# LN2's rows turned on VectorE in 32x32 blocks and carried by 16 small transfers, in a fused attention and FFN kernel

## The chip, the cores and the metric

The kernel runs on one core of a Trainium2 chip. The metric is device time in microseconds (us), the median of several executions. Everything is in float32; a product is made of three TensorE matmuls on "high" and "low" parts of both operands (the high part is rounded to the format that TensorE multiplies in one pass, the low part is the rest).

## What is computed

For each of 16 batches of 512 rows with 512 features, with a context of 77 rows:

```
hc = layernorm(x)                                  # LN1, no gain or bias
sim = hc@w1 + ctx@w2 + (hc*w3)@ctx.T + b_sim ;  A = softmax(sim)
hq = A@ctx ; hbar = softmax(rowmax(sim)) @ hc
x = x + [hc, hq, hc*hq, hc*hbar] @ W_qv + b_qv     # 2048 -> 512
h = layernorm(x) @ W1 + b1                         # LN2, 512 -> 2048
q = h + 0.1*(cos(th)*wr + sin(th)*wi) * wi * sin(th + 0.1*h)
x = x + relu(q) @ W2 + b2                          # 2048 -> 512
```

The change concerns the step from layernorm(x), LN2, to the operand of `@ W1`: TensorE needs the features on the partitions, LN2 has the rows there, so the 512x512 tile has to be turned.

## The kernel before

One program is written by hand for every engine, with counting semaphores between them; the order on each engine is that of the text. The loop is over batches b (0 to 15) and, in each, over 16 tiles f of 128 hidden features. In step f TensorE (PE) makes `hidden(b, f)` (12 matmuls, W1's tile as the weights and `T` as the moving operand) and `second(b, f-3)` (12 matmuls with W2's tile). ScalarE (ACT) reads the PSUM tile `hid` twice (`phase_and_hidden`: `ph`, `h2`), takes the high part of relu (`relu_high`) and the sine; VectorE (DVE) does `reduce_phase`, `sine_term`, `relu_low`. GpSimd (POOL) streams the split weights from DRAM and makes the small row statistics (`moments`). In batch 0 the weights come raw through SyncE's queue (SP), and ACT and DVE split them beside all else (`tile_high`, `tile_low`); SP loads a raw tile only when the low part of the tile two before it is made.

Under the FFN of batch b the attention of batch n = b+1 is made: its large products are put in at f = 10 and 11 (NA = 10), and DVE adds them to `X` (`attention_and_stats`) at f = 11. Then LN2 of batch n follows: `norm_second(n, t)` normalises 128 rows into `xin` on DVE, `tr_second(n, t)` turns them on PE by four 128x128 transposes into the PSUM tile `mis`, `turned_high` (ACT) and `turned_low` (DVE) write them into the half of `T` of the other parity. Rows t = 0, 1 go at f = 13, rows 2, 3 at f = 14. `hidden(n, 0)` waits for `t2_lo`, that is for all of it, at the start of the next batch. `turn_stats(n+1)` is one PE transpose of LN1's statistics for the batch after, at the end of f = 12; `stat_rows` copies it out on ACT, and `spread_stats` sends it over DRAM to all partitions through SP's queue. `ctx_raw` holds the raw context rows of a batch; SP loads it (`ctx_load`) after `spread_stats`.

Of the kernel before, what the change touches and what calls it, by code (L numbers as in the profile page):

```python
# [34 lines left out]
F32 = mybir.dt.float32  # L35
# [15 lines left out]
def xattn_ffn(nc, x, ctx_rows, w_sim, b_sim, W_qv, b_qv, W1, W2, b2, x_turned, ctx_turned, columns, out):  # L51
# [36 lines left out]
    with ExitStack() as ctx:  # L88
# [128 lines left out]
        x2_done = sem("x2_done"); xb2_done = sem("xb2_done")  # L217
        st2 = sem("st2"); mo2 = sem("mo2"); rs2 = sem("rs2"); xn2 = sem("xn2"); tr2 = sem("tr2")
        t2_hi = sem("t2_hi"); t2_lo = sem("t2_lo")
# [110 lines left out]
        x0n = w0_sb  # L330

        g_view = g_raw.rearrange("p (c j) -> p c j", c=C)

# [4 lines left out]
        def _(sp):  # L338
            row = lambda v, n: v.rearrange("(a d) -> a d", a=1).to_broadcast([n, D])

            def x_load(n):

                need(sp, out_stored, 16 * (n - 2))
                sp.dma_start(X[:, n % 3], x_rows[n]).then_inc(x_in, 16)

            def turned_load(n):
# [45 lines left out]
            def ctx_load(n):  # L392

                sp.wait_ge(pr_lo, C * n)
                sp.wait_ge(w0_lo, C * n)
                sp.wait_ge(att_done, RT * n)
                last = chunk_of_row(n * J + J - 1)
                for k in range(chunk_of_row(n * J), last + 1):
                    if k < GAP:
                        sp.wait_ge(p_stored[k % 4], 16 * (k // 4 + 1))  # L400
                    else:
                        sp.wait_ge(p_late[k - GAP], 16)
                g_load(n, ctx_in)
                stack_load(n, hq_raw, hq_tail, ctx_flat, ctx_in)
                stack_load(n, hqw_raw, hqw_tail, hqw_dram, ctx_in)
# [70 lines left out]
            def body(b, par, first, last):  # L476
                n, pn = b + 1, 1 - par
                for f in range(FT):
# [26 lines left out]
                    if f == (NA + 3 if first else NA + 2):  # L505
                        spread_stats(n + 1)

            def rest():
# [9 lines left out]
        def _(pe):  # L518
# [48 lines left out]
            def hidden(b, f, par):  # L567

                g = FT * b + f
                w1_ready(b, f)  # L570
                need(pe, h2_done, g - 1)
                if f == 0:
                    pe.wait_ge(t2_lo, RT * (b + 1))
                if b == 0 and f < 2:
                    pe.wait_ge(c_copy, CN - GAP - 1 + f)
                w = w1s[:, f % NW1]
                for c in range(C):
                    three(hid[:, f % 2], w[:, 0, c], w[:, 1, c], T[:, par, 0, c], T[:, par, 1, c],
                          c == 0, c == C - 1, hid_done if c == C - 1 else None)
# [53 lines left out]
            def sim_rows(n):  # L633
                pe.wait_ge(simt_done, n + 1)
                for t in range(RT):
                    tr = pe.transpose(mis[:, 1, t * J:(t + 1) * J], simt[:, t * P:(t + 1) * P], ident[0:J, 0:J])
                tr.then_inc(simr_done, 1)
# [109 lines left out]
            def body(b, par, first, last):  # L747
                n, pn = b + 1, 1 - par
                for f in range(FT):
# [18 lines left out]
                    if f == NA + 1 and not last:  # L768
                        continue
                    if f == NA + 2 and not last:  # L770
                        second(b, NA - LAG, False)
                        second(b, NA - LAG + 1, False)
# [6 lines left out]
                    if f == NA - 1:  # L779
                        hq_hat(n, 0)  # L780
                    if f == NA + 2 and n + 1 < B:
                        turn_stats(n + 1)
# [15 lines left out]
        def _(sc):  # L798
            def turned_high(n, t, par, ready, done):
                sc.wait_ge(ready, RT * n + t + 1)  # L800
                nc.scalar.copy(T[:, par, 0, :, t * P:(t + 1) * P],
                               mis[:, t % 2].rearrange("p (c r) -> p c r", c=C)).then_inc(done, 1)

            def spread_high(n, c, par):
# [71 lines left out]
            def phase_and_hidden(b, f):  # L876
# [3 lines left out]
                need(sc, q_done, g - 1)  # L880
                nc.scalar.activation(ph[:, f % 2], hid[:, f % 2], ACT.Identity, bias=hbias[:, f:f + 1],  # L881
                                     scale=HSCALE).then_inc(t_done, 1)
                need(sc, act_lo, g - 1)
                nc.scalar.activation(h2[:, f % 2], hid[:, f % 2], ACT.Identity, bias=b1c[:, f:f + 1],  # L884
                                     scale=1.0).then_inc(h2_done, 1)
# [110 lines left out]
            def body(b, par, first, last):  # L996
                n, pn = b + 1, 1 - par
                for f in range(FT):
# [14 lines left out]
                    if f == NA and not last:  # L1013
                        w0_high(n, 1)
                    phase_and_hidden(b, f)
                    if first and f < FT - 3:
                        w1_high(f + 3)
# [27 lines left out]
                    if f == (5 if first else 6):  # L1045
                        max_exponentials(n)
                    if f == NA + 2 and n + 1 < B:
                        stat_rows(n + 1)
                    if f == NA - 1:
# [22 lines left out]
        def _(ve):  # L1072
# [257 lines left out]
            def attention_and_stats(n, tiles=range(RT)):  # L1330

                for t in tiles:
# [3 lines left out]
                    ve.bn_stats(st[:, t], X[:, n % 3, t]).then_inc(st2, 1)  # L1336

            def norm_second(n, t):
                ve.wait_ge(rs2, t // 2 + 1 if isinstance(n, int) and n == 0 else n + 2)
                if t >= 2:  # L1340
                    ve.wait_ge(tr2, RT * n + t - 1)
                ve.tensor_scalar(xin[:, t % 2], X[:, n % 3, t], mv[:, t, 1:2], rstd[:, t:t + 1],
# [106 lines left out]
            def body(b, par, first, last):  # L1449
                n, pn = b + 1, 1 - par  # L1450
                for f in range(FT):
# [10 lines left out]
                    if f == NA + 3 and not last:  # L1462
                        norm_second(n, 0)
                        norm_second(n, 1)
                    if f == NA + 4 and not last:
                        norm_second(n, 2)
                        norm_second(n, 3)
                    reduce_phase(b, f)
# [58 lines left out]
                    if first:  # L1527
                        for p in splits(f, last)[0:1] if f == NA else splits(f, last):
                            tile_low(p)
                    if (f > 0 or not first) and not early:  # L1530
                        relu_low(g - 1, (f - 1) % FT)
# [17 lines left out]
                    if f == NA + 1:  # L1549
                        attention_and_stats(n)  # L1550
                    if f == NA + 3:
                        turned_low(n, 0, pn, t2_hi, t2_lo)
                        turned_low(n, 1, pn, t2_hi, t2_lo)
                    if f == NA + 4:
                        turned_low(n, 2, pn, t2_hi, t2_lo)
                        turned_low(n, 3, pn, t2_hi, t2_lo)

# [176 lines left out]
```

## Time and profile before

| | |
|---|---|
| median of 3 runs | 1956.96 us (1955.17 to 1958.2) |
| profiled execution: its time, its span | 1955.15 us, 1953.3 us |
| PE, DVE, ACT, POOL busy, share of the span | 99%, 71%, 51%, 21% |
| TensorE's granted clock over the run | 0.998 of full speed |

The profiled execution's own time lies 1.8 us below the median. Matmuls overlap in the records (a 512-column matmul is listed with 0.39 us and the next starts 0.23 us later), so times of PE are read from start to start.

### The profile page before, as it was taken

Reading aid. Unit: us, or ns where it says so; the run is one execution under the profiler, and the core shown is the slowest. Engines: PE = TensorE matmul, PEld = TensorE weight load, DVE = VectorE, ACT = ScalarE, POOL = GpSimd, SP = SyncE. Lnnn points to the kernel's source line nnn. Section 1 sums busy time; section 2 is a strip of 40 time slices with the busy share of each in tenths; the row PEclk is TensorE's granted clock in tenths of the full one; section 3 lists DMA queues with packets and bytes.
Section 4 is the critical chain, followed back from the end, with each engine's and each line's share of the span. In section 5 each row is a group of like instructions: output and inputs, shape, how many; then the busy total and the mean of one; then the engine's idle time right before and its main releaser. Section 6 shows DMA issues by size and latency. Waiting matters only on the chain.

```text
span 1953.3 us, 24524 instructions
## 1 busy us (share of the span) xinstructions
PE 1938.4 (99%) x8709; PEld 1585.8 (81%) x8709; DVE 1379.2 (71%) x2377; ACT 990.4 (51%) x1676; POOL 408.4 (21%) x834
## 2 busy tenths in 40 slices
PE   8999999999999999999999999999999999999999
PEld 7778788888888888888888888888888888888887
DVE  7888786766777676776766867667776667767554
ACT  5574645536365363644636455363653636446343
POOL 1223121131211212112121211312122121221210
PEclk9999999999999999999999999999999999999999
DMA  8587857577574875757667475774748757576463
GB/s 258 175 282 244 263 160 238 171 229 226 161 224 141 254 233 164 212 175 226 203 202 222 158 232 166 233 228 159 222 149 253 225 172 213 170 225 189 151 216 119
DMA packets 144279, 397.63 MB, mean 204 GB/s; under 512 B 22380, under 2 KB 35416, under 8 KB 142238
## 3 DMA queue, kind: packets, MB, share of 16 engines
q0 software_dynamic: 83568, 304.29, 49.9%
q1 hardware_dynamic: 60446, 91.74, 15.6%
q8 instruction: 71, 1.16, 0.2%
q14 instruction: 50, 0.41, 0.1%
q10 hardware_dynamic: 144, 0.04, 0.0%
HBM read 355.50 MB, written 38.30 MB: 202 GB/s over the span
## 4 chain that ended last, share of the span: by engine, by line
PE 93%; DVE 3%; ACT 2%; issue 1%; DMA 0%; SPq 0%; DVEq 0%; ACTq 0%
PE acc L521 18%; PE acc L523 17%; PE acc L522 17%; PE hid L521 11%; PE hid L523 11%; PE hid L522 11%; PE mis L607 1%; PE acc L529 1%; PE mis L529 1%; PE acc L530 1%; PE mis L530 1%; PE mis L523 1%; PE mis L521 1%; PE mis L522 1%; DVE ph L1225 0%
## 5 line engine op out<-in xcount | busy, mean ns | idle before, releaser
L521 PE MATMUL hid<-T,w1s 128*128 128x512 f32 x1024 | 403.6, 394 | 3.3 <-ACT h L884 3.3
L521 PE MATMUL acc<-ws,act 128*128 128x512 f32 x1024 | 402.8, 393 | 2.2 <-DVE ws L1082 1.5
L523 PE MATMUL hid<-T,w1s 128*128 128x512 f32 x1024 | 399.8, 390 | 0.0
L522 PE MATMUL hid<-T,w1s 128*128 128x512 f32 x1024 | 399.8, 390 | 0.0
L523 PE MATMUL acc<-ws,act 128*128 128x512 f32 x1024 | 399.2, 390 | 0.0
L522 PE MATMUL acc<-ws,act 128*128 128x512 f32 x1024 | 398.7, 389 | 0.0
L890 ACT ACTIVATE act<-h 128x512 fp32r<-128x512 f32 x256 | 161.9, 633 | 353.7 <-DVE h L1215 332.3
L1223 DVE TENSOR_SCALAR kk<-ph 128x512 f32<-128x512 f32 x256 | 108.7, 425 | 323.0 <-ACT ph L881 323.0
L881 ACT ACTIVATE ph<-hid,hbias 128x512 f32<-128x512 f32 x256 | 175.6, 686 | 279.6 <-PE hid L523 279.2
L1590 POOL DMA_DIRECT2D ws<-w2x_dram x240 | 127.3, 531 | 513.6 <-PE acc L523 504.2
L521 PEld LDWEIGHTS hid<-T,w1s 128*128 128x128 f32 x1024 | 192.9, 188 | 44.9 <-issue 4.1
L1229 DVE SCALAR_TENSOR_TENSOR act<-h,act 128x512 fp32r<-128x512 f32 x256 | 175.9, 687 | 74.6 <-ACT act L890 73.0
L521 PEld LDWEIGHTS acc<-ws,act 128*128 128x128 f32 x1024 | 192.3, 188 | 44.2 <-issue 2.1
L523 PEld LDWEIGHTS hid<-T,w1s 128*128 128x128 f32 x1024 | 192.8, 188 | 40.5
L523 PEld LDWEIGHTS acc<-ws,act 128*128 128x128 f32 x1024 | 192.2, 188 | 40.5
L522 PEld LDWEIGHTS hid<-T,w1s 128*128 128x128 f32 x1024 | 193.1, 189 | 38.7
L522 PEld LDWEIGHTS acc<-ws,act 128*128 128x128 f32 x1024 | 192.4, 188 | 38.8
L1584 POOL DMA_DIRECT2D w1s<-w1x_dram x240 | 129.3, 539 | 452.8 <-PE hid L523 440.9
L1215 DVE SCALAR_TENSOR_TENSOR h<-ph,camp,h 128x512 f32<-128x512 f32 x256 | 191.0, 746 | 0.0
L1225 DVE TENSOR_TENSOR ph<-ph,kk 128x512 f32<-128x512 f32 x256 | 177.3, 693 | 8.8
L884 ACT ACTIVATE h<-hid,cols 128x512 f32<-128x512 f32 x256 | 174.4, 681 | 15.5 <-DVE act L1229 15.5
L894 ACT ACTIVATE ph<-ph 128x512 f32<-128x512 f32 x256 | 158.2, 618 | 1.3 <-DVE ph L1225 1.0
(192 smaller groups left out, 2710.9 us busy)
## 6 DMA issues: line engine op xcount, KB each, us to landing
w1s<-w1x_dram POOLq DMA_DIRECT2D x240, 512.0 KB, 4.4
ws<-w2x_dram POOLq DMA_DIRECT2D x240, 512.0 KB, 4.4
ws<-wqx_dram POOLq DMA_DIRECT2D x56, 512.0 KB, 4.7
full<-in_x_turned SPq DMA_DIRECT2D x15, 1024.0 KB, 4.8
out_x<-X SPq DMA_DIRECT2D x15, 1024.0 KB, 4.7
X<-in_x SPq DMA_DIRECT2D x14, 1024.0 KB, 8.5
w_raw<-in_L_ffn_W SPq DMA_DIRECT2D x32, 256.0 KB, 3.7
w1x_dram<-w1s POOLq DMA_DIRECT2D x16, 512.0 KB, 4.4
```

Of the source, the lines that this page charges most:

```text
L521: pe.matmul(dst, w_hi, m_hi, start=start, stop=False)
L522: pe.matmul(dst, w_hi, m_lo, start=False, stop=False)
L523: mm = pe.matmul(dst, w_lo, m_hi, start=False, stop=stop)
L881: nc.scalar.activation(ph[:, f % 2], hid[:, f % 2], ACT.Identity, bias=hbias[:, f:f + 1], scale=HSCALE).then_inc(t_done, 1)
L884: nc.scalar.activation(h2[:, f % 2], hid[:, f % 2], ACT.Identity, bias=b1c[:, f:f + 1], scale=1.0).then_inc(h2_done, 1)
L890: nc.scalar.activation(act[:, f % 4, 0], h2[:, f % 2], ACT.Relu).then_inc(act_hi, 1)
L894: nc.scalar.activation(ph[:, f % 2], ph[:, f % 2], ACT.Sin, scale=TWO_PI_BELOW).then_inc(s_done, 1)
L1215: ve.scalar_tensor_tensor(out=h2[:, f % 2], in0=ph[:, f % 2], scalar=camp[:, f:f + 1], in1=h2[:, f % 2], op0=ALU.mult, op1=ALU.add).then_i ...
L1225: ve.tensor_tensor(ph[:, f % 2], ph[:, f % 2], kk[:], ALU.subtract).then_inc(r_done, 1)
L1229: ve.scalar_tensor_tensor(out=act[:, f % 4, 1], in0=h2[:, f % 2], scalar=0.0, in1=act[:, f % 4, 0].bitcast(F32), op0=ALU.max, op1=ALU.subtract
L1584: po.dma_start(w1s[:, s].rearrange("p a c k -> p (a c k)"), w1x_dram[f % FT].rearrange("p a c k -> p (a c k)")).then_inc(w1_in[s], 16)
L1590: po.dma_start(ws[:, slot_of(p)], tile_source(p, last, w2x_dram, wqx_dram)).then_inc(w_in[slot_of(p)], 16)
```

## The change

DVE turns each 128 normalised rows in 32x32 blocks (`block_turn`, one instruction) into `ctx_raw`, which is free then. A block is turned in place only, so the blocks still have to move to other partitions: 16 transfers from SBUF to SBUF, of 32 partitions by 512 numbers (64 KB) each, eight on SP's queue (`i` = 0, 1) and eight on ACT's own (`i` = 2, 3), write them into the low half of `T`. ACT then makes the high part from there (`blocks_high`), DVE the low part in place (`blocks_low`). The rows of `T` stand in another order (`T_run`): `hidden` reads four pieces of 128 columns 2 KB apart, and ACT puts the rows back in order as it reads `hid` (`by_groups`, `by_rows`). All this is for batches n = 1 to 15; batch 0 keeps the transposes. `norm_second` moves from f = 13 and 14 to f = 12, `turn_stats` from the end of f = 12 to before its `second` calls.

```
+            def block_moves(n):              # on SP; on ACT the same with i in (2, 3)
+                sp.wait_ge(xb2, RT * n)
+                for i in (0, 1):
+                    for m in range(G):
+                        sp.dma_start(T_run[n % 2][32 * m:32 * m + 32, 1, i].bitcast(F32),
+                                     ctx_raw[32 * i:32 * i + 32, m]).then_inc(t2_in[i], 16)
...
@@ SP, ctx_load
+                for i in range(G):
+                    need(sp, t2_in[i], 16 * G * (n - 1))
...
@@ SP, body
                     if f == (NA + 3 if first else NA + 2):
                         spread_stats(n + 1)
+                    if f == NA + 3:
+                        block_moves(n)
...
@@ PE, hidden
+                    if b == 0:
+                        m, dst = [T[:, par, k, c] for k in range(2)], hid[:, f % 2]
+                    else:
+                        m = [T_run[par][:, k, :, c * P:(c + 1) * P] for k in range(2)]
+                        dst = hid[:, f % 2].rearrange("p (i k) -> p i k", i=G)
...
@@ PE, body
-                    if f == NA + 3:
-                        tr_second(n, 0)
-                        tr_second(n, 1)
-                    if f == NA + 4:
-                        tr_second(n, 2)
-                        tr_second(n, 3)
...
@@ ACT
+            def blocks_high(n, i):
+                sc.wait_ge(t2_in[i], 16 * G * n)
+                nc.scalar.copy(T_run[n % 2][:, 0, i], T_run[n % 2][:, 1, i].bitcast(F32)).then_inc(t2_hi, 1)
...
+                    if f == NA + 3 and not last:
+                        block_moves(n)
                     phase_and_hidden(b, f)
...
                     if f == NA + 3:
-                        turned_high(n, 0, pn, tr2, t2_hi)
-                        turned_high(n, 1, pn, tr2, t2_hi)
+                        blocks_high(n, 0)
+                        blocks_high(n, 2)
                     if f == NA + 4:
-                        turned_high(n, 2, pn, tr2, t2_hi)
-                        turned_high(n, 3, pn, tr2, t2_hi)
+                        blocks_high(n, 1)
+                        blocks_high(n, 3)
...
@@ DVE
+            def block_turn(n, t):
+                ve.wait_ge(xn2, RT * n + t + 1)
+                ve.transpose(blocks[:, :, :, t].rearrange("p m c r -> p c m r"),
+                             xin[:, t % 2].rearrange("p (c m r) -> p c m r", c=C, m=G)).then_inc(xb2, 1)
```

DVE in a later batch, f = 12 to 14. Before, from `reduce_phase` of f = 12 on (`kk` and the first `ph` are its, `h` is `sine_term`, `act` is `relu_low`):

```order
L1223 TENSOR_SCALAR kk<-ph 128x512
L1225 TENSOR_TENSOR ph<-ph,kk 128x512
L1215 SCALAR_TENSOR_TENSOR h<-ph,camp,h 128x512
L1229 SCALAR_TENSOR_TENSOR act<-h,act 128x512
L1342 TENSOR_SCALAR xin<-X,mv,rstd 128x512 x2
L1223 TENSOR_SCALAR kk<-ph 128x512
```

The same place in the change:

```order
L1263 TENSOR_SCALAR kk<-ph 128x512
L1265 TENSOR_TENSOR ph<-ph,kk 128x512
L1255 SCALAR_TENSOR_TENSOR h<-ph,camp,h 128x512
L1393 TENSOR_SCALAR xin<-X,mv,rstd 128x512
L1381 STREAM_TRANSPOSE ctx_raw<-xin 128x4x4x32
L1269 SCALAR_TENSOR_TENSOR act<-h,act 128x512
L1393 TENSOR_SCALAR xin<-X,mv,rstd 128x512
L1381 STREAM_TRANSPOSE ctx_raw<-xin 128x4x4x32
L1393 TENSOR_SCALAR xin<-X,mv,rstd 128x512
L1381 STREAM_TRANSPOSE ctx_raw<-xin 128x4x4x32
```

All four normalisations and four turnings (the last pair is not shown) now stand before `reduce_phase` of f = 13, one pair of them ahead of `relu_low`.

ACT in a later batch, from `relu_high` of f = 12 (`act<-h`) on; `ph<-hid` and `h<-hid` are `phase_and_hidden` of f = 13. Before:

```order
L890 ACTIVATE act<-h 128x512
L894 ACTIVATE ph<-ph 128x512
L811 COPY mean_bc<-mis 12x128
L881 ACTIVATE ph<-hid,hbias 128x512
L884 ACTIVATE h<-hid,cols 128x512
L890 ACTIVATE act<-h 128x512
L894 ACTIVATE ph<-ph 128x512
L801 CAST T<-mis 128x4x128 x2
```

In the change:

```order
L928 ACTIVATE act<-h 128x512
L932 ACTIVATE ph<-ph 128x512
L835 DMA T<-ctx_raw 32x512 x8
L919 ACTIVATE ph<-hid,hbias 128x512
L922 ACTIVATE h<-hid,cols 128x512
L928 ACTIVATE act<-h 128x512
L932 ACTIVATE ph<-ph 128x512
L840 CAST T<-T 128x512 x2
```

Eight DMA issues stand in front of `phase_and_hidden` of f = 13, behind a wait for all four turnings; the statistics' copy has moved ahead.

SP in batch 0, f = 12 to 15, where raw tiles are still loaded. Before:

```order
L417 DMA w_raw<-in_L_ffn_W 128x512 x4
L354 DMA stat_dram<-mean_bc 12x128
L358 DMA mean_bc<-stat_dram 128x512
L358 DMA e_bc<-stat_dram 128x512
L417 DMA w_raw<-in_L_ffn_W 128x512
L376 DMA tmp_w<-in_ctx_turned 128x4x77
```

In the change:

```order
L439 DMA w_raw<-in_L_ffn_W 128x512 x4
L374 DMA stat_dram<-mean_bc 12x128
L378 DMA mean_bc<-stat_dram 128x512
L378 DMA e_bc<-stat_dram 128x512
L363 DMA T<-ctx_raw 32x512 x8
L439 DMA w_raw<-in_L_ffn_W 128x512
L396 DMA tmp_w<-in_ctx_turned 128x4x77
```

SP's eight transfers stand behind the raw loads of f = 13 and behind the three transfers of `spread_stats`.

## Rows read from the trace of the kernel before

**Rows 1.** The page's busy times: us, share of the span, instructions.

```profile
PE 1938.4 (99%) x8709; PEld 1585.8 (81%) x8709; DVE 1379.2 (71%) x2377; ACT 990.4 (51%) x1676; POOL 408.4 (21%) x834
```

**Rows 2.** PE's longest wait: us in total, times, longest.

```profile
PE hid L521 <- ACT h L884: 3.3, 1, 3.3
```

**Rows 3.** Groups by line: busy us, mean ns of one, then idle before.

```profile
L607 PE MATMUL mis<-ident,xin 128*128 128x128 f32 x256 | 33.3, 272 | 0.1
L1082 DVE TENSOR_TENSOR T<-mis,T 128x512 fp32r<-128x512 f32 x68 | 44.0, 686 | 9.7 <-ACT T L801 8.7 <-ACT full L817 0.9
```

**Rows 4.** Timeline of PE in a later batch: start us, us.

```profile
996.66 0.39 PE L521 MATMUL hid<-T,w1s 128*128 128x512 f32 x1
...
999.38 0.39 PE L521 MATMUL acc<-ws,act 128*128 128x512 f32 x1
...
1013.12 1.04 PE L607 MATMUL mis<-ident,xin 128*128 128x128 f32 x8
1013.91 0.48 PE L521 MATMUL hid<-T,w1s 128*128 128x512 f32 x1
...
1016.74 0.39 PE L521 MATMUL acc<-ws,act 128*128 128x512 f32 x1
...
1025.80 0.39 PE L521 MATMUL hid<-T,w1s 128*128 128x512 f32 x1
```

**Rows 5.** Timeline of DVE, ACT and POOL in the same batch.

```profile
1000.10 1.04 POOL L1628 TENSOR_TENSOR rstd<-vareps,mhalf 128x4 f32<-128x4 f32 x1
...
1001.37 0.75 DVE L1215 SCALAR_TENSOR_TENSOR h<-ph,camp,h 128x512 f32<-128x512 f32 x1
...
1010.59 0.69 ACT L881 ACTIVATE ph<-hid,hbias 128x512 f32<-128x512 f32 x1 [2.48 <-PE hid L523]
...
1013.82 0.69 DVE L1229 SCALAR_TENSOR_TENSOR act<-h,act 128x512 fp32r<-128x512 f32 x1 [0.69 <-ACT act L890]
...
1014.22 1.05 ACT L801 CAST T<-mis 128x512 fp32r<-128x512 f32 x2
...
1016.94 0.69 ACT L881 ACTIVATE ph<-hid,hbias 128x512 f32<-128x512 f32 x1 [1.67 <-PE hid L523]
```

**Rows 6.** Issues on SP by line: ns min/median/max, first and last start.

```profile
L344 SPq DMA_DIRECT2D X<-in_x x14: 368/434/891, 131.0 to 1658.1; - x14
...
L387 SPq DMA_DIRECT2D ctx_raw<-in_ctx x16: 252/310/932, 10.2 to 1723.0; - x16
...
L410 SPq DMA_DIRECT2D at_s<-prs x14: 740/751/845, 248.3 to 1785.7; - x14
L411 SPq DMA_DIRECT2D at_s<-prs x14: 792/803/841, 249.2 to 1786.5; - x14
```

**Rows 7.** Timeline of batch 0, f = 12 to 16, all engines.

```profile
164.34 20.97 SPq L417 DMA_DIRECT2D w_raw<-in_L_ffn_W  x4
...
175.56 1.00 DVE L1342 TENSOR_SCALAR xin<-X,mv,rstd 128x512 f32<-128x512 f32 x2
...
180.00 0.69 ACT L881 ACTIVATE ph<-hid,hbias 128x512 f32<-128x512 f32 x1 [2.48 <-PE hid L523]
...
185.35 0.40 SPq L354 DMA_DIRECT2D stat_dram<-mean_bc  x1
...
187.94 0.33 SPq L358 DMA_DIRECT2D mean_bc<-stat_dram  x1
...
188.99 1.08 SPq L417 DMA_DIRECT2D w_raw<-in_L_ffn_W  x1
...
195.19 0.39 PE L521 MATMUL hid<-T,w1s 128*128 128x512 f32 x1
```

**Rows 8.** Timeline of PE in the opening.

```profile
7.11 0.79 PE L521 MATMUL acc<-T,act 128*128 128x512 f32 x1 [1.91 <-DVE act L1082]
...
13.50 0.40 PE L521 MATMUL acc<-T,act 128*128 128x512 f32 x1
```

**Rows 9.** Window of the opening: us, busy by engine, granted clock, DMA share, GB/s.

```profile
8.00:10.00 2.00, 2.00 (x6) 1.48 (x6) 1.82 (x4) 1.36 (x3) 0.00 (x0) 1.00 1.05 384
```

More of the change, by code:

```diff
@@ L217, in xattn_ffn @@
         x2_done = sem("x2_done"); xb2_done = sem("xb2_done")
-        st2 = sem("st2"); mo2 = sem("mo2"); rs2 = sem("rs2"); xn2 = sem("xn2"); tr2 = sem("tr2")
+        st2 = sem("st2"); xb2 = sem("xb2"); t2_in = [sem(f"t2_in{i}") for i in range(4)]; mo2 = sem("mo2"); rs2 = sem("rs2"); xn2 = sem("xn2"); tr2 = sem("tr2")
         t2_hi = sem("t2_hi"); t2_lo = sem("t2_lo")
@@ L330, in xattn_ffn, with by_rows, by_groups @@
         x0n = w0_sb
+        G = P // 32
+        blocks = ctx_raw[:].rearrange("p a d -> p (a d)").rearrange("p (m c t r) -> p m c t r", m=G, c=C, t=RT)
+        T_run = [T[:, q].rearrange("p a c r -> p a (c r)").rearrange("p a (i k) -> p a i k", i=G) for q in range(2)]
+        def by_rows(cols, b):
+            return cols if b == 0 else cols.rearrange("p (t i r) -> p t i r", t=RT, i=G)
+        def by_groups(cols, b):
+            return cols if b == 0 else cols.rearrange("p (i t r) -> p t i r", t=RT, i=G)
         g_view = g_raw.rearrange("p (c j) -> p c j", c=C)
@@ L577, in hidden @@
                 for c in range(C):
-                    three(hid[:, f % 2], w[:, 0, c], w[:, 1, c], T[:, par, 0, c], T[:, par, 1, c],
+                    if b == 0:
[3 more added lines that the diff above has]
+                        dst = hid[:, f % 2].rearrange("p (i k) -> p i k", i=G)
+                    three(dst, w[:, 0, c], w[:, 1, c], m[0], m[1],
                           c == 0, c == C - 1, hid_done if c == C - 1 else None)
@@ L634, in sim_rows @@
                 pe.wait_ge(simt_done, n + 1)
+                need(pe, srow_done, n)
                 for t in range(RT):
@@ L769, in body @@
                         continue
+                    if f == NA + 2 and n + 1 < B:
+                        turn_stats(n + 1)
                     if f == NA + 2 and not last:
@@ L802, in turned_high, with block_moves @@
                                mis[:, t % 2].rearrange("p (c r) -> p c r", c=C)).then_inc(done, 1)
+            def block_moves(n):
+                sc.wait_ge(xb2, RT * n)
+                for i in (2, 3):
+                    for m in range(G):
+                        sc.dma_start(T_run[n % 2][32 * m:32 * m + 32, 1, i].bitcast(F32),
+                                     ctx_raw[32 * i:32 * i + 32, m]).then_inc(t2_in[i], 16)
+            def blocks_high(n, i):
+                sc.wait_ge(t2_in[i], 16 * G * n)
+                nc.scalar.copy(T_run[n % 2][:, 0, i], T_run[n % 2][:, 1, i].bitcast(F32)).then_inc(t2_hi, 1)
             def spread_high(n, c, par):
@@ L1014, in body @@
                         w0_high(n, 1)
+                    if f == NA + 3 and not last:
+                        block_moves(n)
                     phase_and_hidden(b, f)
+                    if f == NA + 2 and n + 1 < B:
+                        stat_rows(n + 1)
                     if first and f < FT - 3:
@@ L1340, in norm_second @@
                 if t >= 2:
-                    ve.wait_ge(tr2, RT * n + t - 1)
+                    ve.wait_ge(xb2 if n else tr2, RT * (n - 1) + t - 1 if n else t - 1)
                 ve.tensor_scalar(xin[:, t % 2], X[:, n % 3, t], mv[:, t, 1:2], rstd[:, t:t + 1],
@@ L1461, in body @@
                         spread_low(n, 3, pn)
[L1462 to L1467, printed above, removed]
+                    if f == NA + 5 and not last:
+                        blocks_low(n, 2)
+                        blocks_low(n, 3)
                     reduce_phase(b, f)
@@ L1529, in body @@
                             tile_low(p)
+                    if f == NA + 2 and not last:
+                        norm_second(n, 0)
+                        block_turn(n, 0)
                     if (f > 0 or not first) and not early:
@@ L1550, in body @@
                         attention_and_stats(n)
-                    if f == NA + 3:
-                        turned_low(n, 0, pn, t2_hi, t2_lo)
-                        turned_low(n, 1, pn, t2_hi, t2_lo)
+                    if f == NA + 2:
+                        for t in range(1, RT):
+                            norm_second(n, t)
+                            block_turn(n, t)
                     if f == NA + 4:
-                        turned_low(n, 2, pn, t2_hi, t2_lo)
-                        turned_low(n, 3, pn, t2_hi, t2_lo)
+                        blocks_low(n, 0)
+                        blocks_low(n, 1)
             def rest():
```

13 lines of the change are left out of this document (7 added, 6 removed).

## The prediction

> **What bounds the kernel now.** I read the page's busy times first: PE is busy for 99% of the span, DVE for 71%, ACT for 51% [rows 1]. Then PE's waits: its longest one is a single 3.3 us [rows 2]; everything else it does is back to back. So PE's own instructions set the time, and what leaves PE is a gain, if nothing that replaces it comes late. Then the timeline of one late batch, from start to start, for what a transpose really costs and for the slack of the chain that LN2 runs through; and last the same places in batch 0, which is the odd one, since ACT, DVE and SP split raw weights there.
>
> **What is removed.** Eight transposes stand between a 512-column matmul and the next: 1013.12 to 1013.91, 0.79 us. The twelve matmuls behind them take 1013.91 to 1016.74, 2.83 us, where an undisturbed dozen takes 996.66 to 999.38, 2.72 us [rows 4]: 0.11 us more. One place costs 0.90 us. There were 256 such transposes in eights [rows 3], 32 places; batch 0's LN2 keeps two, so 30 go: **-27.0 us**. The moved transpose of the statistics costs the same in its new place: 0.
>
> **What hidden's new operand costs.** 15 x 16 x 12 = 2880 matmuls read four pieces of 128 columns in place of 512 in a row. No row shows a moving operand in pieces. From below 0; from above I allow 10 ns each, 29 us. I take 0: a piece is still 512 bytes in a row in each partition. ACT reads hid in pieces too; it idles 1.67 to 2.48 us before each step here [rows 5], so nothing.
>
> **The new chain in a later batch.** The deadline is PE's first matmul of the next batch, 1025.80 [rows 4], less two removed places: 1024.0. The chain, step by step:
> - DVE comes free about 1002.1 (sine term from 1001.37, 0.75), and rstd is there at 1001.1 [rows 5]. Two normalisations are 1.00 us [rows 7], one alone 0.54. The turning has no row. From below 0.54 (that row), from above 1.2 (twice 0.6, if it went at half the rate of an ordinary pass). I take the ordinary pass of 512 numbers, 0.69 [rows 3], about 0.64 from start to start: a pair is 1.2 us. One pair, relu_low 0.6, three pairs: all turned at 1007.5. DVE's next work before needed ph of f = 13, from 1010.59 [rows 5], so DVE loses nothing.
> - ACT waits for that and issues eight transfers. Behind this wait stands ph of f = 13, which before began at 1010.59 [rows 5]. The price of one issue is what decides. From below 0.31 us (51 rows into SBUF), in between 0.43 us (a 1 MB load over 128 partitions); from above 0.75 and 0.80 us, the two at_s moves, the only ones that go from SBUF to SBUF as these do [rows 6]. Those have 51 and 26 rows, these 32, which like the 128 of the 1 MB load divide evenly over 16 DMA engines. I take 0.38 with the gap, between the first two: 3.0 us, ph at 1010.7, a delay of 0.1.
> - ph of f = 14 is ready when PE is: 1016.94 less one place, 1016.0; ACT itself is free 4.7 us after ph of f = 13 (casts from 1014.22 to 1015.27 against 1010.59 [rows 5]), 1015.4, if the blocks have landed. SP's first four are issued by 1009, and with 2.6 us from issue to landing (the write of the statistics, 185.35 to 187.94 [rows 7]) they have.
> - relu_low of that step starts 3.23 us after ph (1013.82 - 1010.59 [rows 5]); it and four low parts at 0.61 are 3.1 us, with the semaphore 6.4: T complete at 1022.4. **Slack 1.6 us, cost 0.** It is gone when ph of f = 13 is later than 1012.9, that is from 0.67 us per issue on.
>
> The Trainium skill, "DMA: Bandwidth & Descriptors", section "Why a DMA increments its semaphore by 16 and not by 1", says that a hardware-issued DMA uses the largest number of engines up to 16 that divides its slowest dimension, and that the issuing sequencer itself writes the increments that are left. By it the at_s moves use 3 and 13 engines, and ours 16. That would speak for the short issue, but the 51-row load at 0.31 us [rows 6] has leftovers too, so the trace does not bear it out. The skill's "VectorE: DVE Perf Modes", section "The three transpose paths", gives 311 ns for 128x128 in 2-byte numbers; four of these would make an estimate of 1.24 us a turning, all turned at 1009.7, and with 0.38 us an issue the chain would still be in time.
>
> **Batch 0.** Here the same chain is late. DVE's first pair starts at about 175.3 and all is turned at 180.7 (one pair, 0.6, three pairs, as above; before, the normalisations stood at 175.56 [rows 7]). Eight issues put ph of f = 13 at 183.7 in place of 180.00: 3.7 us late. SP's last raw load of f = 13 ends at 185.31 [rows 7]: it waits for a low part that ACT and DVE make after this very ph, so it slips by 3.7 us too. Then come the statistics, and SP is free for its moves only at 188.99 + 3.7 = 192.7. The fourth is issued 1.1 us later and lands 2.6 us after that: 196.4. ACT sits in blocks_high until then, casts two (1.1), ph of f = 14 at 197.5. From there 6.4 us as above, and 1.7 for the raw tile's high and low parts that stand in the same step: T complete at 205.6. PE is ready at 195.19 [rows 7] less 1.8, 193.4: **+12.2 us**, once. From below, issues that cost nothing: SP free at 188.99, complete at 200.9, +7.5.
>
> After 12 us of idling PE may also restart slowly. In the opening, after an idle stretch of 1.91 us, it took 7.11 to 13.50 for 15 matmuls [rows 8], 0.43 us each where 0.227 is its pace later: 3.0 us lost. The granted clock is listed as 1.00 there [rows 9], so by that column it would be no matter of the clock; the pace says otherwise. Between 0 and 3.0 I take **+2 us**.
>
> **Sum.** -27.0 + 12.2 + 2 = -12.8 us against the profiled execution's 1955.15: 1942.4; the median lies 1.8 us above that execution: **1944 us**. With issues at 0.31 to 0.6 us, landings at 2 to 5 us and the restart at 0 to 3, this case's own range is 1938 to 1951.
>
> **Rivals.**
> - *An issue costs what the at_s moves cost.* For it: they are the nearest kind, and steady at 0.74 to 0.85 us over 28 issues [rows 6]. Against it: only their odd sizes. At 0.83 with the gap eight are 6.6 us: ph of f = 13 at 1014.1, of f = 14 at 1018.8, T at 1025.2 against 1024.0, a stall of 1.2 us in each of 14 batches, 17 us; batch 0: 187.3, SP free at 196.3, landed at 201.4, T at 210.6, +17.2 and the restart's 2. Sum -27.0 + 17 + 19.2 = +9, **1966 us**, 1957 to 1976. From about 0.76 us an issue the change is a loss.
> - *Batch 0 costs nothing*, because SP gets to its moves earlier than I read. Then -27, **1930 us**. Against it: three issues of rows 7 stand ahead in SP's order, and each is tied to another engine.
> - *The pieces cost TensorE something.* 10 ns a matmul gives 1944 + 29 = **1973 us**; it turns the sign from 4.4 ns on. Nothing in the trace speaks for or against.
> - *In between*: issues near 0.7 us, or turnings at the half rate with issues of 0.6: **1950 to 1958**.
>
> **How the numbers follow.** My forecast has 0.50, the dear issues 0.32, a free batch 0 0.06, costly pieces 0.05, in between 0.07. About 0.2% (4 us) is what a measurement of this kernel can tell from no change. Faster takes the first, the third and part of the last: 0.59. Same, 1953 to 1961, takes the rest of the last and the lower edge of the dear issues: 0.09. Slower 0.32. The range goes from 1936, inside the free case's side, to 1971, over most of the dear issues.
>
> **What would show it.** The eight issues on ACT's queue in a late batch: near 0.38 us or near 0.8. PE's waits at hid of the first tile of a batch: one of about 12 us near 193 and none later is my forecast; fifteen, fourteen of them about 1 us, the main rival. ph of f = 14 in batch 0 held back by t2_in of SP's first four. The twelve matmuls of hidden at 2.72 us. Wrong would make me a turning far over 0.69 us, landings of 64 KB over 5 us under the weight stream, or a pace of hidden other than 0.227 us.

## The result, and the profile after

The changed kernel takes 1969.9 us (median of 4, 1966.88 to 1977.13), the kernel before 1956.24 (4 runs): ratio 1.0078, 95% interval 1.0063 to 1.0092. It is 0.8% slower, where I had forecast 1944 us. The profiled execution is the one of 1977.13 us, span 1975.2, 7.2 us above the median, so its stalls are larger than the median's.

The page's busy times, against [rows 1]:

```profile
PE 1924.1 (97%) x8469; PEld 1559.4 (79%) x8469; DVE 1414.5 (72%) x2437; ACT 989.5 (50%) x1676; POOL 409.0 (21%) x834
```

The 240 transposes are gone from PE and it is 14.3 us less busy, but the span is longer: idle time of PE went from 14.9 us to 1975.2 - 1924.1 = 51.1. The groups of waits (us in total, times, longest) say whom PE and ACT wait for, against [rows 2]:

```profile
PE hid L547 <- DVE T L1122: 29.6, 11, 16.3
...
ACT T L840 <- DMA T<-ctx_raw: 28.7, 17, 12.9
```

One wait of 16.3 us is batch 0's; the other 13.3 us are spread over ten later batches. Behind them stand ACT's waits for the small transfers, 12.9 us in batch 0 and 15.8 in later ones. The new operations, each by its line of the kernel: the first row is the turning (busy us, mean ns, idle before); the next are the issues (ns min/median/max, first and last start), then the us from issue to landing on ACT's queue (SP's has the same median):

```profile
L1381 DVE STREAM_TRANSPOSE ctx_raw<-xin 128x512 f32<-128x512 f32 x60 | 42.7, 711 | 2.1
...
L835 ACTq DMA_DIRECT2D T<-ctx_raw x120: 514/614/1381, 182.0 to 1864.0; - x120
...
L363 SPq DMA_DIRECT2D T<-ctx_raw x120: 522/607/1567, 196.1 to 1864.4; - x120
...
DMA to landing us min/median/max: 2.0/7.2/11.5
```

**A late batch.** The timeline of DVE, ACT and PE in a late batch, against [rows 5] and [rows 4]:

```profile
1027.05 0.71 DVE L1381 STREAM_TRANSPOSE ctx_raw<-xin 128x512 f32<-128x512 f32 x1
1027.79 5.06 ACTq L835 DMA_DIRECT2D T<-ctx_raw  x8
1032.95 0.69 ACT L919 ACTIVATE ph<-hid,hbias 128x512 f32<-128x512 f32 x1 [9.00 <-issue]
...
1037.03 1.14 ACT L840 CAST T<-T 128x512 fp32r<-128x512 f32 x2 [0.35 <-DMA T<-ctx_raw]
...
1042.35 1.15 ACT L840 CAST T<-T 128x512 fp32r<-128x512 f32 x2 [0.56 <-DMA T<-ctx_raw]
1044.55 0.47 PE L547 MATMUL hid<-T,w1s 128*128 128x512 f32 x1
```

The last turning ends at 1027.76, and ACT needs 5.06 us for its eight issues, not 3.0; `ph` of f = 13 starts 5.2 us after the last turning. Between 1020 and 1060 us the transfers take 7.1 us on both queues, and DVE completes T at 1044.41, just as PE wants it. From the last turning to a complete T it is 16.65 us here; over thirteen later batches it is 16.2 to 19.3, and PE wants T 16.6 us after that turning. So it ends in a stall or not, batch by batch. Windows (us, busy by engine, granted clock, DMA share, GB/s) show what it comes to; first twelve batches of before:

```profile
297.43:1718.43 1421.00, 1421.00 (x6409) 1166.10 (x6408) 1004.62 (x1716) 719.58 (x1212) 303.88 (x624) 1.00 0.66 202
```

and the same twelve of after, with PE's waits in them, then ten us behind each of three stalls, of 2.75, 2.18 and 2.18 us:

```profile
309.98:1734.14 1424.16, 1409.95 (x6218) 1144.78 (x6217) 1032.71 (x1764) 718.99 (x1214) 304.63 (x625) 1.00 0.73 210
...
PE hid L547 <- DVE T L1122: 11.6, 8, 2.7
PE mis L668 <- ACT tmp_w L937: 1.2, 7, 0.2
...
690.00:700.00 10.00, 10.00 (x38) 8.14 (x39) 9.02 (x12) 4.22 (x8) 1.06 (x2) 0.85 0.69 191
...
1282.30:1292.30 10.00, 10.00 (x37) 8.09 (x38) 9.14 (x12) 4.27 (x8) 1.05 (x2) 0.83 0.72 213
1640.40:1650.40 10.00, 10.00 (x44) 8.28 (x45) 9.06 (x12) 5.27 (x10) 1.58 (x3) 1.00 0.86 235
```

The period was 1421.00/12 = 118.42 us and is 118.68; less two places at 0.90 it should have been 116.62, so 2.06 us are given back in each. PE, never idle in these batches before, is idle for 1424.16 - 1409.95 = 14.2 us, most of it (11.6) in waits for T.

It is also busy longer than it need be for the same matmuls: 1409.95 us, where the best kernel below takes 1399.79. Only a part of those 10.2 us is the clock. Behind the stalls of 2.75 us (which ends at 689.86) and of 2.18 (1282.28) the granted clock is 0.85 and 0.83 over ten us, and the next step of hidden and second takes 7.05 and 7.17 us in place of 5.44: 3.3 us in all. Behind the other stall of 2.18 us (1640.39) and behind all shorter ones (0.3 to 1.5 us) it stays at 1.00. The rest was not followed to its end; part of it is the way that stalls are listed. A matmul's record runs 0.16 us beyond the start of the next one, so a stall costs 0.16 us more than its idle time, and a short wait such as those of `mis` for `tmp_w` shows only in part.

**Batch 0.** Its timeline, against [rows 7]:

```profile
181.96 5.09 ACTq L835 DMA_DIRECT2D T<-ctx_raw  x8
187.15 0.69 ACT L919 ACTIVATE ph<-hid,hbias 128x512 f32<-128x512 f32 x1 [11.28 <-issue]
...
192.51 0.40 SPq L374 DMA_DIRECT2D stat_dram<-mean_bc  x1
...
193.37 0.50 PE L547 MATMUL acc<-ws,act 128*128 128x512 f32 x1 [1.80 <-DVE act L1269]
...
196.09 5.45 SPq L363 DMA_DIRECT2D T<-ctx_raw  x8
...
204.83 1.14 ACT L840 CAST T<-T 128x512 fp32r<-128x512 f32 x2 [12.92 <-DMA T<-ctx_raw]
...
213.97 0.76 PE L547 MATMUL hid<-T,w1s 128*128 128x512 f32 x1 [16.26 <-DVE T L1122]
...
218.97 0.39 PE L547 MATMUL acc<-ws,act 128*128 128x512 f32 x1
```

SP comes to its moves at 196.09, behind the raw loads and the statistics; ACT sits in `blocks_high` for 12.92 us meanwhile, and PE stalls for 1.80 us and then for 16.26. The first dozen of hidden then takes 213.97 to 218.97, 5.0 us instead of 2.72. Windows of these stretches:

```profile
194.00:198.00 4.00, 3.71 (x11) 2.37 (x9) 0.00 (x0) 0.00 (x0) 0.07 (x1) 0.59 1.03 361
198.00:214.00 16.00, 0.03 (x1) 0.06 (x1) 5.66 (x10) 6.16 (x11) 1.61 (x3) 0.61 0.60 185
214.00:218.00 4.00, 4.00 (x10) 3.13 (x11) 3.97 (x6) 1.66 (x3) 0.00 (x0) 0.50 0.86 260
```

The mean granted clock is 0.59 in the window before the long stall, which follows waits of 0.72 and 1.80 us, and 0.50, the lower level of 1.2 GHz, for the four us behind the stall. The slow dozen before the stall (from 193.37) cost nothing, since PE then had to wait for T in any case; the one behind it cost 5.0 - 2.72 = 2.3 us.

From the statistics' transpose of batch 0 to that of batch 1 it is 140.11 us, before 120.17: 19.9 us more. Since this stretch also lost two places, 1.8 us, what batch 0 costs by itself is 21.7.

### The profile page after: what moved, and what is told of

It reads as the page before. It is cut to its first block, busy times and chain, and to the rows that moved or that the text cites. A ratio compares the mean times of both kernels' runs of the same rounds, so it can differ in the third digit from the quotient of the medians.

```text
span 1975.2 us, 24327 instructions
## 1 busy us (share of the span) xinstructions
PE 1924.1 (97%) x8469; PEld 1559.4 (79%) x8469; DVE 1414.5 (72%) x2437; ACT 989.5 (50%) x1676; POOL 409.0 (21%) x834
## 3 DMA queue, kind: packets, MB, share of 16 engines
q1 hardware_dynamic: 66206, 99.61, 17.9%
## 4 chain that ended last, share of the span: by engine, by line
PE 55%; DVE 20%; ACT 9%; DMA 8%; issue 6%; SPq 2%; ACTq 1%; DVEq 0%
PE acc L547 11%; PE acc L549 10%; PE acc L548 10%; PE hid L547 7%; PE hid L549 6%; PE hid L548 6%; DMA T<-ctx_raw 5%; DVE h L1255 3%; DVE ph L1265 3%; DVE T L1122 3%; ACT ph L919 2%; DVE kk L1263 2%; DVE act L1269 2%; DVE xin L1393 1%; DVE full L1148 1%
## 5 line engine op out<-in xcount | busy, mean ns | idle before, releaser
L547 PEld LDWEIGHTS hid<-T,w1s 128*128 128x128 f32 x1024 | 193.8, 189 | 81.3 <-issue 41.1
```

Of the source, the lines that this page charges most:

```text
L547: pe.matmul(dst, w_hi, m_hi, start=start, stop=False)
```

## The experiments

My theory after the result had three parts: the PE time saved is real; batch 0 costs 20 us; in the later batches the price of an issue and the landing time together use up the slack. The rivals: the saving itself is smaller than read (pieces of `hid`'s operand, clock), or one of issue and landing alone explains the later batches. The kernel before was timed anew beside each group of runs (1955.7, 1956.68 and 1955.68 us). "turned by PE for n = 1" below means that only batch 0's place keeps the old way; these kernels have 28 of the 30 places.

**Is a transpose worth 0.1 us?** The kernel before, with one transpose of four in `tr_second` for n of 1 and more (180 fewer):

```
-                for c in range(C):
+                for c in range(1 if done is tr2 and n else C):
```

> The kernel before, with one of the four transposes of each 128 rows instead of four in batches 1 to 15 (three quarters of the turned operand are left out). Theory (each place costs 0.90 us of TensorE, of which 0.79 is the transposes themselves): 180 transposes fewer at 0.1 us are 18 us, 1938 us. Rival (transposes are hidden or cost only their listed overlap): above 1950 us.

Measured: 1937.34 us (4 runs) against 1955.7, ratio 0.9903 (0.9887 to 0.9920): 18.4 us for 180, 0.102 us each, as expected. The saving is as read.

**What batch 0 costs.** The changed kernel, with batch 1's rows (made under batch 0) turned by PE as before:

```
-            return cols if b == 0 else cols.rearrange(...)
+            return cols if b <= 1 else cols.rearrange(...)
...
-                    if f == NA + 3:
+                    if f == NA + 3 and n > 1:
                         block_moves(n)
```

> The changed kernel, but the LN2 rows made in batch 0 go by TensorE's transposes as before (16 more transposes), so only batches 2 to 15 use the blocks. Theory (the loss sits in batch 0, where SP's moves queue behind the raw weight loads): batch 0 loses its 22 us and gives back 1.8, the time is near 1950 us. The later batches by themselves then show what they make of 14 x 1.8 us saved: in the changed kernel their period was 118.68 us against 118.42 before, so nothing is left and the result should be within 4 us of before. Rival (the loss is spread over all batches, by a cost of the pieces or of the block path itself): 1965 us or more.

Measured: 1949.77 us (10 runs, 1946.19 to 1958.07) against 1955.7, ratio 0.9971 (0.9957 to 0.9984). So the change in batch 0 loses 1969.9 - 1949.8 = 20.1 us in the medians, as its timeline said (19.9). In the later batches 5.9 us are gained instead of the 25.2 that 28 places at 0.90 should give: they take back 19.3 us, 1.4 a batch, and not quite all as I had expected. (The profile of this kernel is of its execution of 1956.13 us, 6.4 above its median.)

**Is it SP's order in batch 0?** The changed kernel, with SP's moves of batch 0 at the start of f = 13, ahead of the raw loads and the statistics:

```
+                    if first and f == NA + 3:
+                        block_moves(n)
                     if first:
...
-                    if f == NA + 3:
+                    if f == NA + 3 and not first:
                         block_moves(n)
```

> The changed kernel with one step moved: in batch 0 SP issues its eight moves at the start of f = 13, ahead of the raw loads and of the statistics. Theory (ACT's wait of 12.9 us in blocks_high of batch 0 is SP's order): SP issues at 182, the blocks have landed by 190, the long stall of TensorE at 214 shrinks from 16.3 us to about 8, and the time is 8 to 12 us below the changed kernel's, near 1960. Rival (the wait is the transfers' own landing): no change, 1968 to 1970.

Measured: 1958.25 us (10 runs, 1952.72 to 1962.97), ratio 1.0007 (0.9996 to 1.0019). Of the 20 us, 11.7 are gone, as expected. The timeline of batch 0, SP and PE:

```profile
180.27 5.40 SPq L363 DMA_DIRECT2D T<-ctx_raw  x8
...
199.27 0.77 PE L549 MATMUL hid<-T,w1s 128*128 128x512 f32 x1 [4.58 <-DVE T L1124]
```

The stall is 4.58 us in place of 16.26. SP's order was the larger part. What is left over the kernel with batch 1 turned by PE is 8.5 us; ACT's own issues, the chain behind them and the slow clock (0.67 and 0.65 over 195 to 205 us) are there to account for it, but they were not tried one by one.

**Size of the transfers.** The kernel with batch 1 turned by PE, and 64 of 512 columns in each move (8 KB in place of 64, so most of T is stale); SP's moves, and ACT's likewise:

```
-                        sp.dma_start(T_run[n % 2][32 * m:32 * m + 32, 1, i].bitcast(F32),
-                                     ctx_raw[32 * i:32 * i + 32, m]).then_inc(t2_in[i], 16)
+                        sp.dma_start(T_run[n % 2][32 * m:32 * m + 32, 1, i, 0:64].bitcast(F32),
+                                     ctx_raw[32 * i:32 * i + 32, m, 0:64]).then_inc(t2_in[i], 16)
```

> As e1_b0_old, but each move carries 64 of its 512 columns (8 KB in place of 64 KB; the rest of the turned operand is stale), with the same number of issues. Theory A (what holds the later batches is the landing of the moved bytes beside the weight stream): landings fall from 7.1 us to under 4 and the stalls vanish, 14 x 1.8 us come out, near 1930. Theory B (what holds them is ACT's 5.1 us of issuing ahead of its reading of hid): about the same time as e1.

Measured: 1937.85 us (4 runs) against 1955.7, ratio 0.9908 (0.9893 to 0.9923), 11.9 us under the same kernel with full moves. The waits, first with full moves and then with small ones, and the landing of the small:

```profile
PE hid L547 <- DVE T L1136: 12.1, 11, 2.7
...
ACT T L846 <- DMA T<-ctx_raw: 13.4, 13, 2.0
```

```profile
PE hid L547 <- DVE T L1136: 2.4, 4, 0.8
...
DMA to landing us min/median/max: 3.0/4.0/5.8
```

The number of issues is the same in both, the landing 7.2 and 4.0 us. PE's waits for T fall from 12.1 to 2.4 us. The time lies between the two that I had named (1930 and 1950), nearer to the theory of landing: without the long landing the dear issues are nearly in time. The four waits that are left stand in the four batches where ACT's eight issues took longest, 5.8 to 6.2 us, not 5.0.

**Issue apart from landing.** ACT issues none; its eight moves are issued on POOL's queue, which has room (21% busy), at the start of f = 13:

```
+                    if f == NA + 3 and not last and n > 1:
+                        po.wait_ge(xb2, RT * (n - 1))
+                        for i in (2, 3):
+                            for m in range(G):
+                                po.dma_start(T_run[n % 2][32 * m:32 * m + 32, 1, i].bitcast(F32),
+                                             ctx_raw[32 * i:32 * i + 32, m]).then_inc(t2_in[i], 16)
```

> As e1_b0_old, but the eight moves that ACT issued stand on POOL's queue, at the start of f = 13, so nothing stands in front of ACT's reading of hid. Theory B (in the later batches ACT's 5.1 us of issuing, which puts ph of f = 13 at 2 us behind its input, is half of the loss): ph starts when PE is ready, T is complete 2 us earlier unless a landing is later than that; 1938 to 1944. Theory A (only the landings hold it): ACT now waits in blocks_high instead, 1948 to 1951, the same as e1.

Measured: 1952.2 us (10 runs, 1948.12 to 1957.57) against 1956.68, ratio 0.9977 (0.9966 to 0.9988): no gain over the kernel with ACT's issues, and above both values that I had named. PE's stall at hidden's first tile is gone, but others came, four steps later. The waits, then a late batch:

```profile
PE acc L547 <- DVE X L1380: 8.0, 12, 0.8
PE mis L547 <- DVE T L1134: 6.0, 7, 2.4
...
DVE e_bc L1259 <- DMA ctx_raw<-hqw_dram: 46.5, 13, 5.7
```

```profile
1011.06 4.09 POOL L1757 DMA_DIRECT2D T<-ctx_raw  x8 [6.05 <-DVE ctx_raw L1393]
1015.14 0.58 POOL L1662 DMA_DIRECT2D w1s<-w1x_dram  x1
1015.70 1.62 POOL L1668 DMA_DIRECT2D ws<-w2x_dram  x3
...
1042.22 0.69 DVE L1259 CUSTOM_DVE_ANT_0 e_bc<-ctx_raw,w_bc 77x512 f32<-77x512 f32 x1 [3.46 <-DMA ctx_raw<-hqw_dram]
```

The 46.5 us are a new wait of DVE, for the next batch's context rows, just ahead of DVE's `X` that PE then waits for (8.0 us); the `mis` of the attention products waits for 6.0 more, on LN1's part of `T`. It is natural to think that `ctx_raw`, which the change borrows for the turned rows, comes free late. It doesn't: these loads start 12.9 us behind the last turning here (1010.76 to 1023.69) and 14.9 in the kernel with ACT's issues (1005.91 to 1020.82). They land late. POOL waits 6.05 us for the last turning and issues moves for 4 more, with the weight loads held up behind them; six of those then go at once (1015.14 to 1018.4), and weight loads still take long to land when the context rows are loaded. The issues and landings of 512 KB weight loads while the context loads are under way, here over 1024 to 1043 us:

```profile
w1s<-w1x_dram POOLq DMA_DIRECT2D x4, 512.0 KB, 7.1
ws<-w2x_dram POOLq DMA_DIRECT2D x3, 512.0 KB, 7.1
```

and in the kernel with ACT's issues, over 1020 to 1037:

```profile
w1s<-w1x_dram POOLq DMA_DIRECT2D x3, 512.0 KB, 4.6
ws<-w2x_dram POOLq DMA_DIRECT2D x3, 512.0 KB, 4.9
```

One wait took the place of another. In this kernel the moves land fast on both queues, in 2.4 us on POOL's and in 2.7 on SP's (medians), since the weight loads stand behind POOL's wait. The same with 64 of 512 columns a move (T mostly stale):

> As e5_pool_issues, with moves of 64 of the 512 columns (8 KB; the rest of the operand stale). Issue time and bytes are both out of the chain: 1930 to 1934, the ceiling of the later batches. If it is not below e4_b0_old_small (1937.85), ACT's issuing cost nothing there, and what is left over 1930 is something else.

Measured: 1939.85 us (4 runs) against 1956.68, ratio 0.9918 (0.9904 to 0.9933), landings 1.6 to 1.9 us. Expected were 1930 to 1934; it missed, and it is no better than small moves with ACT's issues (1937.85). DVE's new wait is there too, 27.8 us in 13 times: POOL is held up by the turning whatever the size of the moves. So relief for ACT, bought with a hold-up of POOL, gave nothing as long as the pairs of normalisation and turning come late.

**The pairs earlier.** The kernel with batch 1 turned by PE, and all four pairs of normalisation and turning right behind `reduce_phase` of f = 12, so that the last turning is done sooner:

```
                     reduce_phase(b, f)
+                    if f == NA + 2 and not last and n > 1:
+                        for t in range(RT):
+                            norm_second(n, t)
+                            block_turn(n, t)
```

> As e1_b0_old, but all four pairs of normalising and turning stand right behind reduce_phase of f = 12, ahead of sine_term and relu_low, so all moves are issued about 1.2 us earlier. If the later batches are late at the end of one chain (turn, issue, land, split), whatever link is the dear one, each batch with a stall gives back up to 1.2 us: 1938 to 1943. If the stall is caused by relu_low or sine_term alone: no change or worse.

Measured: 1943.93 us (4 runs) against 1956.68, ratio 0.9934 (0.9918 to 0.9949), 5.8 us under the same kernel with late pairs, and 0.9 above the range that I had named. In a late batch the last turning ends 17.8 us ahead of hidden's first matmul (999.54 to 1017.33); with late pairs it is 16.7, a stall of 0.94 taken off. That is the 1.1 us that the new place was to give, and stalls are left. PE's waits for T, and twelve batches as a window:

```profile
PE hid L547 <- DVE T L1136: 3.4, 8, 0.8
...
290.04:1699.12 1409.08, 1403.95 (x6218) 1143.71 (x6217) 1033.80 (x1764) 719.62 (x1213) 305.52 (x625) 1.00 0.72 213
```

**Both.** Early pairs and ACT's moves on POOL's queue, for engineers who want the version to keep:

> e5 and e6 together. If both shorten the same chain, the stalls at hid of tile 0 are gone and the 14 batches give their full 1.8 us: 1930 to 1936. If POOL's queue delays the landings (weights stand in the same queue), no better than e6.

Measured: 1931.07 us (4 runs, 1929.41 to 1933.70) against 1956.68, ratio 0.9872 (0.9857 to 0.9886). It leaves nothing of the computation out and is 1.3% faster than the kernel before. Twelve batches as a window, and a late batch:

```profile
289.49:1689.28 1399.79, 1399.79 (x6218) 1145.92 (x6217) 1036.13 (x1764) 719.81 (x1214) 353.85 (x721) 1.00 0.70 214
```

```profile
995.08 3.97 POOL L1754 DMA_DIRECT2D T<-ctx_raw  x8 [4.80 <-DVE ctx_raw L1393]
999.17 0.69 ACT L925 ACTIVATE ph<-hid,hbias 128x512 f32<-128x512 f32 x1 [2.56 <-PE hid L549]
...
1008.45 2.50 DVE L1134 TENSOR_TENSOR T<-T 128x512 fp32r<-128x512 f32 x4
...
1012.57 0.39 PE L547 MATMUL hid<-T,w1s 128*128 128x512 f32 x1
```

`ph` of f = 13 waits 2.56 us for `hid` as before, not for issues; T is complete at 1010.95, 1.6 us ahead of PE, and POOL's moves land in 2.3 us (median). DVE's wait for the context rows is down to 13.5 us in 11 times and reaches PE no more. PE is busy in all of the twelve batches: 1399.79/12 = 116.65 us each, 1.77 under before, where two places at 0.90 are 1.80. Against this window the kernel with early pairs alone has 9.3 us more, 5.1 of them idle; its granted clock is 1.00 in these batches, so there the slow clock has no part. By steps, 5.8 of the 9.3 us lie at hidden's first tile and right behind it, and 3.4 in the step where `mis` waits for `tmp_w`, which the best kernel does not do; why ACT is late there was not followed up.

**Landing alone, the other way.** POOL's weight loads of f = 13 wait until the moves have landed, so that these run undisturbed; with ACT issuing its own moves again, on late pairs and on early pairs:

```
+                    if f == NA + 3 and not last and n > 1:
+                        for i in range(G):
+                            po.wait_ge(t2_in[i], 16 * G * (n - 1))
```

> As e1_b0_old (ACT issues its eight moves itself), with one wait added: at f = 13 POOL sends its next weight loads only when all moves of the batch have landed. It tells what the gain of e7 came from. If the landing beside the weight stream (7.2 us against 2 to 3 when nothing is queued) is the whole of it: landings of 3 us, T in time, about e5's 1952 or better, since the weights and the context loads come later. If ACT's 5.1 us of issuing matters by itself: stalls of about 0 to 1 us at hid of tile 0 stay, 1945 to 1950.

> The same wait on top of e6_pairs_early. Landing theory: it comes down to e7's 1931 with ACT still issuing. Issuing theory: it stays at e6's 1944 or within 3 us of it.

Measured: 1969.85 us (4 runs) against 1955.68, ratio 1.0076 (1.0061 to 1.0091), and 1958.46 (10 runs), ratio 1.0014 (1.0005 to 1.0024). Both lie above all that I had expected. As times they say only that weights held back cost more than they give, but the trace of the first shows the chain without the weights beside it:

```profile
1011.47 6.36 ACTq L841 DMA_DIRECT2D T<-ctx_raw  x8
1017.93 0.69 ACT L925 ACTIVATE ph<-hid,hbias 128x512 f32<-128x512 f32 x1 [10.30 <-issue]
...
1026.42 2.49 DVE L1136 TENSOR_TENSOR T<-T 128x512 fp32r<-128x512 f32 x4
...
PE acc L547 <- DMA ws<-w2x_dram: 29.8, 13, 6.3
...
DMA to landing us min/median/max: 2.0/2.1/3.9
```

The same 64 KB moves land in 2.1 us (median) when no weights stream (128 GB/s over 1011.5 to 1018 us), and in 7.2 when they do. No wait for T at hidden's first tile is left on PE, but that alone proves little, because PE now stands for `ws` just before it. In the batch shown T is complete at 1028.91, 17.5 us after the last turning, though no landing was waited for: the eight issues alone took 6.36 us. Without its wait for `ws` PE would have wanted T at 1028.0.

**The chain, kernel by kernel.** In each trace the chain can be read in thirteen later batches: from the end of the last turning to `ph` of f = 13, from there to `ph` of f = 14, and in all to a complete T; last, how long after the turning PE wants T when nothing delays it (us, least to most).

| kernel | to `ph`, f = 13 | to `ph`, f = 14 | to T | wanted |
|---|---|---|---|---|
| late pairs, ACT issues (batch 1 by PE) | 5.2 to 6.4 | 4.7 to 6.8 | 16.4 to 19.3 | 16.6 |
| the same, small moves | 5.2 to 6.4 | 4.7 | 16.1 to 17.4 | 16.6 |
| the same, weights held | 5.2 to 6.5 | 4.7 | 16.1 to 17.5 | 16.6 |
| late pairs, POOL issues | 3.1 | 5.4 | 14.9 | 16.6 |
| early pairs, ACT issues | 5.8 to 6.9 | 4.7 to 6.5 | 16.9 to 18.6 | 17.8 |
| the same, weights held | 5.8 to 6.9 | 4.7 | 16.8 to 17.9 | 17.8 |
| early pairs, POOL issues | 4.4 | 5.4 | 16.2 | 17.8 |

It shows both terms at work. The issues take all of the slack with late pairs but for 0.4 us, and more in the batches where eight of them last 6 us and not 5. The landings then add up to 2.1 us in the second column. Where neither is in the way, the chain is the same in every batch and 1.6 us early. With late pairs and POOL's issues T comes in time too, and what that kernel loses, it loses at the waits four steps later.

## Why the prediction was wrong

**Right.** What PE gains: 0.90 us a place (0.102 a transpose by experiment, 1.77 us a period in the best kernel). The pieces of hidden's operand at 0: in after the dozen of hidden takes 2.72 us (1033.42 to 1036.14), and the period of 116.65 against 116.62 leaves them nothing. The turning, 0.69 forecast, 0.71 measured. The place of batch 0's stall, and SP's queue order as its main cause.

**The step that failed** is "Slack 1.6 us, cost 0" in the later batches: the chain that replaces the transposes was priced too short in two of its terms, the issue and the landing. Batch 0's 12.2 us come out too small by the same two.

**Failed: the price of an issue.** I took 0.38 us with the gap, against the at_s moves at 0.75 and 0.80, the nearest kind in [rows 6], because those have odd sizes. It is 0.61 us, 0.65 from start to start: between 0.38 and 0.83 (with the gap), and nearer to the one that I argued away. By my own chain that put `ph` of f = 13 only 2 us later and the threshold was 0.67, so by itself it left T just in time: 5.2 us to `ph`, 4.7 to the next step, 6.4 to T complete is 16.3 us from the last turning at 1007.5, against a deadline 16.5 after it. The slack was 0.2 us where I had written 1.6 (0.4 in the traces where nothing waits for a landing). And the eight issues do not always take their 5.0 us: with 6 the slack is gone.

**Failed: the landing.** I took 2.6 us from the write of the statistics [rows 7]. It is 7.2. That row stands in a quieter stretch (213 GB/s over 185.3 to 188 us); the moves go out while POOL streams 512 KB weight loads (305 GB/s over 1028 to 1034 us, in the late batch above). I named a landing above 5 us as what would make me wrong, but read no row of a transfer in that very stretch. With hardly any slack left, ACT's waits for it (15.8 us in the later batches of after) come out as PE stalls (13.3 us).

**Left out: the clock after a stall.** I had reckoned a slow restart only in batch 0, and there 2.3 us were measured where I took 2. In the later batches it is a small term: of the 1424.16 - 1399.79 = 24.4 us that twelve batches of after have over the same of the best kernel, the slow pace behind two stalls is 3.3. By steps, 13.5 us lie in the step that ends with hidden's first matmul, 4.2 in the one behind it (the 3.3 are in these), and 6.8 in three places later in the batch that I did not follow up. What I read from the opening, a pace of 0.43 us under a listed clock of 1.00, stays unexplained: behind batch 0's stall the pace was 0.42 and the clock was listed with 0.50.

**Batch 0, mis-sized.** 14.2 us forecast, 21.7 measured. The issues (5.09 us in place of 3.0) put SP at its moves at 196.09 and not at 192.7. Its fourth is issued about 198 and not 193.8, and it lands beside other traffic (361 GB/s over 194 to 198 us), so ACT casts at 204.83 and not at 196.4. T is complete at 213.8, 8.2 us later than forecast.

**The sum.** In the medians: -27.0 as forecast; +21.9 for batch 0 (20.1, and the 1.8 of its two places) where I had 14.2; +19.3 given back in the later batches where I had 0. That is +14.2, and 13.7 are measured. In the profiled executions, which lie 22.0 us apart, it is -27.0 + 21.7 + 14 x 2.06 = +23.5, 1.5 too much, which I can't place. My rival of dear issues, with 1.2 us a batch and a sum of 1966 us, came nearest, in part by luck: it put the whole 1.2 on an issue of 0.83 and kept the landing at 2.6.

**What stays open.** The chain to T is accounted for by the table above, but not the whole time of each kernel. Moving the issues from ACT to POOL gave nothing with late pairs (+2.4 us) and 12.9 us with early ones. That the bunched weight loads are what cancelled the gain with late pairs is read from the traces (DVE's waits for context rows of 46.5 and 13.5 us, weight landings of 7.1 against 4.6 and 4.9) and was not tried by itself. In the kernels with POOL's issues two things change at once, ACT is free and the moves have no weight loads beside them; small moves and held weights show the second alone, but a kernel with only the first was not made. All batches in the new way, batch 0 with the last kernel's order, were not tried either.

## What to carry to other kernels

A transfer's price is its issue on the queue's engine and its landing beside what streams then; take both from rows of the same kind and the same stretch, and doubt an argument for leaving the nearest row. If work leaves the engine that bounds the kernel, the chain that replaces it wants slack for its slow batches and not for its median one: here the same chain took 16.2 to 19.3 us. And where small transfers are bound to come beside bulk loads, start their producers early and let the small ones go first; the bulk loads are held back meanwhile, and a kernel can lose as much there as it gained.

## What the runs showed of the hardware

- Sixteen DMAs on two queues at once, SBUF to SBUF, 32 x 512 f32 each: 0.61 us an issue on SP's and on ACT's queue (medians; 0.51 to 1.57); with 51 and 26 partitions before 0.75 and 0.80. On POOL's queue an issue of the same took 0.50.
- Such a move lands in 2.1 us (median) while the weight loads are held, in 7.2 beside weight loads of 512 KB, in 4.0 there when it has 8 KB. With POOL issuing half of them ahead of its weight loads it was 2.3 to 2.4 on POOL's queue and 2.7 to 2.8 on SP's.
- TensorE's granted clock had a mean of 0.59 over four us after waits of 0.72 and 1.80 us, and was 0.50 for four us behind a stall of 16.26. In late batches of the changed kernel it was 0.85 and 0.83 over the ten us behind stalls of 2.75 and 2.18 us, and 1.00 behind another of 2.18 and behind those of 0.3 to 1.5.
- A matmul whose moving operand is four pieces of 512 bytes keeps the pace of one run of 2 KB, 0.227 us.
